# The second sub-layer's last additions, divided between VectorE and ScalarE with GpSimd

## What is computed

```
x = x + tanh(g_xattn[0]) * _L0_xattn_ref(ctx, ctx, _layernorm(x), ...)
x = x + tanh(g_ffn[0]) * _L0_ffn_ref(_layernorm(x, axis=-1), sim_matrix, gates, w_q, w_k, w_v, o_weights)
x = x + tanh(g_xattn[1]) * _L1_xattn_ref(_layernorm(x, axis=-1), ctx, ctx)
x = x + tanh(g_ffn[1]) * _L1_ffn_ref(_layernorm(x, axis=-1), w_router, w_fc, w_proj)

def _L0_ffn_ref(hidden_states, ...):
    routing, mask, fallback_count = _gating(hidden_states, sim_matrix, gates)
    v_all = jnp.einsum('btc,ehc->bteh', hidden_states, w_v)
    combined = jnp.einsum('be,bteh->bth', routing, v_all * mask[:, None, :, None])
    w_o_dyn = jnp.einsum('be,ehd->bhd', routing, o_weights)
    return jnp.einsum('bth,bhd->btd', combined, w_o_dyn)
```

## Time and profile before

| what | value |
|---|---|
| time, median of 3 runs | 1681.53 us (1680.91 to 1683.77) |
| the profiled execution's own time | 1682.86 us |
| its span in the trace | 1681.1 us |
| the loop of eight steps in it: first addition to last root | 506.21 to 554.23 us |
| TensorE, VectorE, ScalarE, GpSimd busy over the span | 91%, 74%, 58%, 61% |

### The profile page before, as it was taken

How to read it: one execution, slowest core, us unless ns; L and a number is a source line. 1 busy time by engine, 2 the same in 40 slices (tenths; PEclk the granted TensorE clock), 3 DMA queues, 4 the chain that set the end, 5 groups by cost and what they waited for, 6 DMA issues and landing times.

```text
span 1681.1 us, 28191 instructions
## 1 busy us (share of the span) xinstructions
PE 1531.7 (91%) x8674; PEld 1054.5 (63%) x8674; DVE 1250.4 (74%) x1795; ACT 967.7 (58%) x1523; POOL 1021.2 (61%) x965
## 2 busy tenths in 40 slices
PE   5999999996676599999999999886999999999996
PEld 4677777775442244444444444366998999999985
DVE  7688888888538578888888887245677777777774
ACT  6333333325422167777778777745677676777763
POOL 4788888874203367887787787700355555555553
PEclk9999999998789589999999999987999999999998
DMA  6344444427452847677776764292244444444443
GB/s 248 114 139 139 143 140 142 137 102 202 100 154 72 194 118 191 184 181 190 189 184 180 197 186 133 70 331 102 51 76 76 76 79 81 80 76 76 76 77 50
DMA packets 110842, 224.24 MB, mean 133 GB/s; under 512 B 12704, under 2 KB 12704, under 8 KB 109856
## 3 DMA queue, kind: packets, MB, share of 16 engines
q1 hardware_dynamic: 94848, 185.88, 38.6%
q0 software_dynamic: 15904, 37.23, 12.7%
HBM read 146.71 MB, written 75.84 MB: 132 GB/s over the span
## 4 chain that ended last, share of the span: by engine, by line
PE 36%; DMA 23%; issue 3%; DVE 2%; ACT 1%; POOL 1%; SPq 0%; POOLq 0%; DVEq 0%; ACTq 0%
DMA out_rows<-XN,slots 21%; PE pB L1377 10%; PE pA L1359 8%; PE pO L1387 8%; PE pO L1400 4%; PE pO L1538 1%; DMA XN<-normed_rows,slots 1%; PE pO L1510 1%; PE pA L1527 1%; PE pB L1368 1%; PE pA L1449 1%; POOL out_rows L1343 1%; PE pB L1475 1%; PE pA L1456 1%; DVE low L1710 1%
## 5 line engine op out<-in xcount | busy, mean ns | idle before, releaser
L1710 DVE TENSOR_REDUCE low<-pA 128x2 f32<-128x1024 f32 x256 | 306.7, 1219 | 86.5 <-PE pA L1359 77.0
L1608 ACT ACTIVATE pt<-pB 128x512 f32<-128x512 f32 x512 | 290.0, 593 | 105.3 <-PE pB L1377 102.9
L430 PE MATMUL y<-kv,toep 128*128 128x288 f32 x1280 | 327.8, 413 | 9.0 <-DVEq L63 5.8
L1343 POOL DMA_INDIRECT out_rows<-XN,slots x71 | 196.8, 2772 | 216.0 <-DMA out_rows<-XN,slots 166.3
L430 PEld LDWEIGHTS y<-kv,toep 128*128 128x128 f32 x1280 | 239.1, 191 | 97.5 <-DVEq L63 34.1
L1527 PEld LDWEIGHTS pA<-XN,fc 128*128 128x128 f32 x2272 | 267.2, 193 | 7.7 <-ACT fc L1667 1.2
L1527 PE MATMUL pA<-XN,fc 128*128 128x128 f32 x2272 | 267.9, 277 | 1.7 <-DVE XN L1871 1.7
L1377 PE MATMUL pB<-qs,ks 98*128 98x512 f32 x512 | 229.1, 451 | 2.7 <-ACT pt L1608 2.4
L1377 PEld LDWEIGHTS pB<-qs,ks 98*128 98x128 f32 x512 | 97.0, 191 | 186.8 <-ACT pt L1608 121.9
L1359 PE MATMUL pA<-ks,qs 96*128 96x512 f32 x512 | 196.2, 428 | 19.5 <-DMA qs<-q_low 17.3
L400 ACT ACTIVATE ym<-y 128x384 f32<-128x384 f32 (+1 forms) x128 | 52.5, 410 | 230.7 <-PE y L430 230.7
(11 more groups left out here) (262 smaller groups left out, 2443.6 us busy)
## 6 DMA issues: line engine op xcount, KB each, us to landing
ks<-ctx_high SPq DMA_DIRECT2D x64, 256.0 KB, 5.0
qs<-q_high SPq DMA_DIRECT2D x64, 256.0 KB, 7.0
kc<-in_ctx_conv SPq DMA_DIRECT2D x32, 384.0 KB, 5.5
XN<-in_x SPq DMA_DIRECT2D x16, 512.0 KB, 9.8
toep<-kernel_and_skip SPq DMA_DIRECT2D x32, 256.0 KB, 3.5
ct<-in_ctx SPq DMA_DIRECT2D x16, 512.0 KB, 6.7
ctx_high<-kh SPq DMA_DIRECT2D x16, 512.0 KB, 4.4
ctx_low<-kl SPq DMA_DIRECT2D x16, 512.0 KB, 5.2
```

The lines of the kernel that those rows point to most:

```text
L430: m = pe.matmul(y[half].rearrange("p (l n) c -> p l n c", l=CB)[:, l, :, 0:PAIRS], toep[u][:, (l - s) * P:(l - s + 1) * P], kv[u][:, half, ...
L1343: pool.indirect_dma_start(out=out["out"], out_offset=bass.IndirectOffsetOnAxis(ap=slots[:, j:j + 1], axis=0), in_=ys[j % 2], in_offset=Non ...
L1608: act.activation(pt[s][:, h, :], bank(u, n), ACT.Exp, scale=SCALE1).then_inc(s_exp, 1)
L1710: dve.tensor_reduce(ap(low[u % 2], t % CB * NH + t // CB, [[NH, 2], [1, 1]]), pA[n % 2], op=ALU.max, axis=AX.X, negate=True).then_inc(s_re ...
```

## The change

The additions of the rows with even n (the first of each double bank) stay on VectorE. Those with odd n, 16 of 32, are taken apart: ScalarE's `scaled` multiplies the PSUM result by `gr` into one of two SBUF buffers `part`, and GpSimd's `add_row` adds the buffer to the row. VectorE looks at row n-3 while it adds row n, and closes row n-4. TensorE's `outer` waits for `s_x1` and `s_part` (the result read out by ScalarE), VectorE's look at an odd row for `s_sum` (GpSimd's addition). `hidden` stands one step earlier in ScalarE's queue. Since semaphores are limited, `s_wz` of the next block goes, and `s_one` counts for it.

```diff
@@ gpsimd, the loop's part
+                def add_row(n):
+                    j = ROUND[2 * n + 1]
+                    pool.wait_ge(s_part, n + 1)
+                    if j < HELD:
+                        pool.wait_ge(s_back, 16 * (HELD // TH))
+                    pool.tensor_tensor(row(j), row(j), part[n % 2], ALU.add).then_inc(s_sum, 1)
+
+                for n in range(TH):
+                    add_row(n)
                 next_roots(0)
                 for s in range(PAIRSB):
+                    for n in range(TH * s + TH, min(TH * s + 2 * TH, UNITS // 2)):
+                        add_row(n)
                     if ORDER[s] == 0:
                         low(0)
                     if s + 1 < PAIRSB:
                         next_roots(s + 1)
                     if ORDER[s] == 0:
                         low(1)
@@ tensor, outer
-                        after(s_x1, pe, UNITS + 2 * (n - 2))
+                        after(s_x1, pe, UNITS + n - 2 if n > 2 else 0)
+                        after(s_part, pe, n - 2)
@@ vector
-                for n in range(UNITS + 2):
-                    sums(n, 1, lambda n: py[n // 2 % 3][n % 2], lambda n: gr[:, ROUND[n]:ROUND[n] + 1], lambda n: ROUND[n],
-                         s_py, lambda n: 2 * (n // 2) + 2)
+                def addition(n):
+                    j = ROUND[n]
+                    dve.wait_ge(s_py, n + 1)
...
+                    dve.scalar_tensor_tensor(row(j), py[n // 2 % 3][0], gr[:, j:j + 1], row(j), ALU.mult, ALU.add).then_inc(s_x1, 1)
+
+                def look(n):
+                    if n % 2:
+                        dve.wait_ge(s_sum, n // 2 + 1)
+                    else:
+                        dve.wait_ge(s_x1, UNITS + n // 2 + 1)
+                    dve.wait_ge(s_mv, UNITS + n - 2)
+                    dve.bn_stats(st6[(UNITS + n) % 3], row(ROUND[n])).then_inc(s_bn, 1)
+
+                def close(n):
+                    dve.wait_ge(s_bn, UNITS + n + 1)
+                    dve.bn_aggr(mv[1][:, n, :], st6[(UNITS + n) % 3]).then_inc(s_mv, 1)
+
+                for n in range(UNITS + LAG):
+                    if n < UNITS and n % 2 == 0:
+                        addition(n)
+                    if n >= LAG - 1 and n - LAG + 1 < UNITS:
+                        look(n - LAG + 1)
+                    if n >= LAG:
+                        close(n - LAG)
@@ scalar
+                def scaled(n):
+                    j = ROUND[2 * n + 1]
+                    act.wait_ge(s_py, 2 * n + 2)
+                    after(s_sum, act, n - 1)
+                    act.activation(part[n % 2], py[n % 3][1], ACT.Copy, scale=gr[:, j:j + 1]).then_inc(s_part, 1)
+
                 hidden(0)
                 hidden(1)
+                for n in range(TH):
+                    scaled(n)
+                if PAIRSB > 2:
+                    hidden(2)
+                for n in range(TH, 2 * TH):
+                    scaled(n)
                 roots(LAST + 1, 1, 0, 4)
                 for s in range(PAIRSB):
-                    if s + 2 < PAIRSB:
-                        hidden(s + 2)
+                    if s + 3 < PAIRSB:
+                        hidden(s + 3)
+                    for n in range(TH * s + 2 * TH, min(TH * s + 3 * TH, UNITS // 2)):
+                        scaled(n)
@@ the next block, gpsimd and sync
-            sp.wait_ge(s_wz, 1)
+            sp.wait_ge(s_one, 1)
...
-            pool.memset(wr, 0.0).then_inc(s_wz, 1)
-            pool.wait_ge(s_wz, 1)
+            pool.memset(wr, 0.0).then_inc(s_one, 1)
+            pool.wait_ge(s_one, 1)
```

More of the change, by code:

```diff
@@ L514, in _build @@
             wo = [ap(room, i * C, [[1, C]]) for i in range(4)]
+            part = [ap(room, (4 + i) * C, [[1, C]]) for i in range(2)]
             st6 = [sb(st, f"st3_{i}", [P, 6]) for i in range(3)]
@@ L551, in _build @@
             (s_con, s_in4, s_act, s_e0, s_ot, s_t1, s_x1, s_bn, s_mv, s_t2, s_ev, s_gs, s_rs, s_srm, s_ctr, s_dve, s_pe,
-             s_sr, s_rm, s_rb, s_wp, s_wd, s_wp2, s_wa, s_hold, s_wo, s_back, s_pc, s_cb, s_py, s_q, s_ql, s_st) = [
+             s_sr, s_rm, s_rb, s_wp, s_wd, s_wp2, s_wa, s_hold, s_wo, s_back, s_pc, s_cb, s_py, s_q, s_ql, s_st, s_part, s_sum) = [
                 sem(n + "_3", st) for n in (
@@ L555, in _build @@
                     "s_srm", "s_ctr", "s_dve", "s_pe", "s_sr", "s_rm", "s_rb", "s_wp", "s_wd", "s_wp2", "s_wa", "s_hold",
-                    "s_wo", "s_back", "s_pc", "s_cb", "s_py", "s_q", "s_ql", "s_st")]
+                    "s_wo", "s_back", "s_pc", "s_cb", "s_py", "s_q", "s_ql", "s_st", "s_part", "s_sum")]
             s_wst = [sem(f"s_wst3{i}", st) for i in range(2)]
@@ L563, in _build @@
             STEPS = 7
+            LAG = 4
             def row(j):
@@ L893, in _ @@
                                     ).then_inc(s_wd, 1)
-                for n in range(UNITS + 2):
-                    sums(n, 1, lambda n: py[n // 2 % 3][n % 2], lambda n: gr[:, ROUND[n]:ROUND[n] + 1], lambda n: ROUND[n],
-                         s_py, lambda n: 2 * (n // 2) + 2)
+                def addition(n):
+                    j = ROUND[n]
+                    dve.wait_ge(s_py, n + 1)
+                    if j < HELD:
+                        dve.wait_ge(s_back, 16 * (HELD // TH))
+                    dve.scalar_tensor_tensor(row(j), py[n // 2 % 3][0], gr[:, j:j + 1], row(j), ALU.mult, ALU.add).then_inc(s_x1, 1)
[16 more added lines that the diff above has]
+                        close(n - LAG)
             @block.scalar
@@ L1082, in _build @@
         pN = pO[1][:, C - E1:]
-        (s_t, s_ev, s_l, s_lg, s_m, s_gap, s_e2, s_took, s_pos, s_in, s_R, s_w, s_dve, s_cnt, s_Q, s_V, s_W, s_pl, s_wz,
+        (s_t, s_ev, s_l, s_lg, s_m, s_gap, s_e2, s_took, s_pos, s_in, s_R, s_w, s_dve, s_cnt, s_Q, s_V, s_W, s_pl,
          s_slots) = [
             sem(n + "_7", st) for n in ("s_t", "s_ev", "s_l", "s_lg", "s_m", "s_gap", "s_e2", "s_took", "s_pos",
-                                        "s_in", "s_R", "s_w", "s_dve", "s_cnt", "s_Q", "s_V", "s_W", "s_pl", "s_wz", "s_slots")]
+                                        "s_in", "s_R", "s_w", "s_dve", "s_cnt", "s_Q", "s_V", "s_W", "s_pl", "s_slots")]
         xc, ys = ([ap(XN, (3 + 2 * n + i) * C, [[1, C]]) for i in range(2)] for n in range(2))
@@ L1246, in _ @@
         def _(pool):
-            pool.memset(wr, 0.0).then_inc(s_wz, 1)
-            pool.wait_ge(s_wz, 1)
+            pool.memset(wr, 0.0).then_inc(s_one, 1)
+            pool.wait_ge(s_one, 1)
             pool.memset(ones, 1.0).then_inc(s_one, 1)
             for u in range(4):
-                pool.wait_ge(s_one, u + 1)
+                pool.wait_ge(s_one, u + 2)
                 pool.memset(ks[u][NS:P], 1.0).then_inc(s_one, 1)
-            pool.wait_ge(s_one, 5)
+            pool.wait_ge(s_one, 6)
             def constants():
@@ L1435, in _ @@
             maxima(0, pB[1])
-            pe.wait_ge(s_one, 5)
+            pe.wait_ge(s_one, 6)
             for t in range(2 * LEAD):
```

## The result

| | before | after |
|---|---|---|
| time, median of 4 runs each | 1682.58 us (1680.91 to 1683.77) | 1698.28 us (1698.22 to 1698.72) |
| ratio | | 1.0095 [1.0077, 1.0112] |
| span of the profiled execution | 1681.1 us | 1697.0 us |
| TensorE's first `outer` of the loop to the end of the last roots | 505.01 to 554.23 = 49.22 us | 502.96 to 570.30 = 67.34 us |

The change makes the kernel 15.7 us slower. The same kernel measured again on another occasion gave 1697.47 us against 1679.83 for the kernel before, ratio 1.0113 [1.0086, 1.0140], so 17.6 us. The forecast was 1700.2 us.

The account below looks back on a forecast made before the run. VectorE was taken to bound the loop, at 5.27 us per four rows. With rings of 7.49 us and slower later steps the loop ends 18.7 us later, giving 1700.2 us for the median, range 1694 to 1707.

Parts of the forecast that it names:

- step 4: Loop step normalising the first two batches: roots, two additions, second scaling, normalisation to `low(0)`, and `low(0)` take 10.5 us.
- the step behind it: Loop step after step 4: roots, `low(1)`, then addition to guess take 9.9 us.
- the last group: Loop's last stretch between roots: roots, addition, hand-over, looks, closes and guess take 6.3 us, to 570.9.
- The ring: Loop: GpSimd's roots and addition, VectorE's looks and closes, ScalarE's guess take turns, 7.49 us per four rows against 5.27.
- The start: Loop's start up to the first group's roots: 514.3 against 514.22 before, so nothing is gained there.
- what the loop's end moves, the whole time moves: Barrier behind the loop: no load of the next block can start ahead of it, so the loop's delay passes on whole.
- The copy of `cb`: One step earlier in ScalarE's queue: removes VectorE's wait of 2.91 us, but saves nothing, since VectorE waits for GpSimd there.
- hold each other up: Rival in the loop: GpSimd's second addition blocks VectorE's looks, 1.28 us a ring, 9 us, 1709; chance 0.05.
- The clock: Rival: TensorE's clock falls to half in the loop, its step 0.4 us above the ring, 1702; chance 0.08.
- VectorE's relief: Rival: GpSimd's additions run ahead, its 41.4 us bound the loop, which ends 5.8 us earlier, 1675.7; chance 0.05.
- VectorE's waits: Loop: VectorE idle for about 3.5 us in each step, ended by GpSimd's addition, where it had none.
- The sum: Loop's terms added up: it ends at 572.9 against 554.23, 18.7 us later.

Follow-up runs that it names:

- Half an addition: Changed kernel with GpSimd adding only the first 256 of 512 columns of each odd row: 1693.68 us, ratio 1.0074.
- a close moved up: Changed kernel with the close of each fourth row directly behind its look, ahead of the next look: 1697.03 us, ratio 1.0094.
- the whole reordering: Changed kernel with four of GpSimd's additions ahead of the first roots instead of two, then two a step: 1678.95 us, ratio 0.9985.
- moving the subtractions: Changed kernel with `low(0)` and `low(1)` each one step later, behind GpSimd's additions: 1695.06 us, ratio 1.0091.
- the gathered kernel: Changed kernel with GpSimd's roots in two goes, 20 rows behind 14 additions, 12 behind the last two and both subtractions: 1666.79 us, again 1668.0.

## Why the prediction was right, step by step

The forecast's sum beside the trace of the kernel after, counted from the start of the first `outer` (505.01 in the profile before):

| term | forecast, us | measured, us |
|---|---|---|
| first `outer` to the roots of group 0 | 9.3 | 9.68 |
| four rings | 4 x 7.49 = 29.96 | 29.54 |
| step 4 | 10.5 | 10.30 |
| the step behind it | 9.9 | 9.68 |
| the last group | 6.3 | 6.20 |
| its roots | 1.95 | 1.94 |
| sum | 67.9 | 67.34 |

The terms' errors partly cancel: the start was 0.4 us too short, all that follows together 0.95 too long.

- **The ring** was the deciding step, and it is there in every bracket. Its parts: roots 2.02 (forecast 2.01), first addition and hand-over 1.30 (1.32), VectorE 3.24 (3.28), close to Ln 0.20 (0.19), Ln to roots 0.62 (0.69). The term of 0.69 was the one mis-sized: it was read between 518.80 and 519.49, and is 0.62 in every ring here. Half an addition, a close moved up and the whole reordering each changed the ring by what these parts say.
- **The start** was too short. The forecast let the first result of a bank pair out 0.7 us after its `outer` starts; in the kernel after it takes 1.17:

```profile
502.96 1.99 PE L756 MATMUL pk<-room,cb 64*128 64x512 f32 x8
...
504.13 1.61 DVE L913 SCALAR_TENSOR_TENSOR XN<-pk,gr,XN 128x512 f32<-128x512 f32 x2 [4.82 <-PE pk L756]
```

  Half of the pair's duration left out the time from the last product to its consumer. It cost about 0.4 us, once.
- **Step 4 and the next**, where the scalings hold up the normalisation, this one `low(0)`, and both `low` the next additions: 0.2 us off each, and confirmed by moving the subtractions. The same run qualifies the forecast's "what the loop's end moves, the whole time moves": that holds only while the stores have landed by then (561.02 against 570.30 in the kernel after).
- **The copy of `cb`** earned nothing in the new loop, as the waits that end by GpSimd show; alone in the kernel before, it takes 3 us off the loop.
- **VectorE and GpSimd do not hold each other up.** Looks take 0.69 us and additions 0.72 beside GpSimd's additions, as before, and GpSimd's additions take 1.27 on average, as the 1.28 of the earlier trace rows. In the gathered kernel's steady 20 us GpSimd is busy for 13.48 and VectorE for all 20, and VectorE keeps 3.95 us a step. The rival is refuted. The Trainium skill's narrower rule (SBUF — State Buffer, section SBUF: two separate sides) gives the contention to VectorE instructions with two SBUF inputs or in a two-port mode; those here have one input in SBUF, and the trace agrees.
- **The clock** did fall, 0.83 in the window of the steady part against 1.00 before, and at no cost. TensorE's group for one bank pair went from 1.13 to 2.08 us within the loop:

```profile
520.27 1.13 PE L756 MATMUL pk<-room,cb 64*128 64x512 f32 x4 [0.40 <-ACT cb L991]
...
542.42 2.08 PE L756 MATMUL pk<-room,cb 64*128 64x512 f32 x4 [2.15 <-ACT cb L991]
```

  but the rings stayed at 7.38 and 7.39. The rival had the cause right and its price wrong. It put TensorE's whole work of a step, `inner` and `outer`, at half clock for all the remaining steps. But the clock came back in between (a group took 1.13 us again at 529.78), and when it fell for good, ahead of 542.42, TensorE had no `inner` left, since it runs them two steps ahead: one step's two groups of 2.08 us fit into any ring. The recorded reading of the first fall is a little off too: the clock did not fall after the wait of 5.8 us but within it, as the 0.81 of that very stretch shows.
- **VectorE's relief** was refuted by 2.1 us a ring. The condition named for it, a ring under 5.27 us, is what the reordering fulfils (4.61), and then it does come out on the other side, by 3.2 us of loop where that rival had 5.8.
- **VectorE's waits** were forecast as about 3.5 us and are 3.3; GpSimd's ahead of its roots, some 3 us, are 2.87.
- **The sum.** The loop was forecast 18.7 us longer and is 18.1. The time is 15.7 and 17.6 us longer in the two measurements. For the profiled execution the forecast was 1701.6; take off 0.6 for the loop and 2.05 for the earlier start of the first `outer`, add 0.8 for the next block's loads, take off 1.0 for the rest, and it is 1698.8, where 1698.72 was measured. So of the 2.9 us only 0.6 are the sum's own error; the others lie outside the loop, in code that the change does not touch, and that they are so small is luck.

## What to carry to other kernels

Before work is taken off the busiest engine, it has to be clear where in the receiving engine's queue it will stand. Follow the waits once round: if the next piece of moved work stands behind an instruction that waits for what another engine makes of the piece before, the engines take turns, and the sum of busy time says nothing. The cure is order, not amount: run the moved work a group ahead (21 us of loop against the kernel after, for two lines, though against the kernel before the time shows no clear gain), or gather the small dependent instructions at the end of the loop. Here the gathered version beats the kernel before by 0.6 to 0.7%; 7.2 us of it are the loop, and some 4.6 us a clock that came back early for no known reason. And look at what else has to be done at the loop's end: in both kernels with late subtractions the store of their result, not the last roots, held up the next block.

## What the runs showed of the chip

- The granted clock of the block behind the loop came back from 0.50 after 21.7 us in both profiles of the gathered kernel, and after 33.5 to 36.9 us in the eight profiles of all the others. The block's scores take 3.6 to 5.4 us less with it. So it seems to depend on something in the kernel ahead of that block. On what is open, and I had not expected a block's first 20 us to be equal in every column and its clock to differ afterwards.
- A lower clock need not cost anything: 0.83 in the loop, and the same ring to 0.01 us.
- Untouched code differs between executions. The kernel before spans 1670.70 to 1686.77 us over all its runs, and the 32 matmuls of `inner` ahead of the first `outer` took 3.67 us at full clock in some profiles and 5.2 at a mean clock of 0.69 in others. A loop's change of 3 us is plain in the trace (46.2 against 49.2) and lost in the medians.
